# Edge messages summed per destination window on one Trainium2 core: strips and a fold replaced by one PSUM sum

## What is computed

```python
w_ij  = silu(edge_feats @ rad_W1 + rad_b1) @ rad_W2 + rad_b2
w_ij += silu(chi_scalar @ sph_W1 + sph_b1) @ sph_W2 + sph_b2
q_i = (node_feats @ Wq)[receivers];  k_j, v_j = (node_feats @ Wk)[senders], (node_feats @ Wv)[senders]
alpha = (q_i * w_ij * k_j).sum(axis=-1) / sqrt(16) * cutoffs      # per head: 8 heads of 16
out = segment_sum(alpha * v_j, receivers, num_segments=n_nodes) / 16
x = layernorm(x + out)
```

## Time and profile before

| | us |
|---|---|
| median of three runs (2751.88 to 2758.18) | 2755.45 |
| the profiled execution's own time | 2762.11 |
| its span, from the first to the last instruction | 2760.2 |
| TensorE busy (matmuls) | 1905.8 |
| TensorE's weight loads, which overlap matmuls | 1496.6 |
| VectorE busy | 1581.1 |
| GpSimd busy | 1537.5 |
| ScalarE busy | 712.5 |

### The profile page before, as it was taken

How to read it: one execution, slowest core, us unless ns; L and a number is a source line. 1 busy time by engine, 2 the same in 40 slices (tenths; PEclk the granted TensorE clock), 3 DMA queues, 4 the chain that set the end, 5 groups by cost and what they waited for, 6 DMA issues and landing times.

```text
span 2760.2 us, 40664 instructions
## 1 busy us (share of the span) xinstructions
PE 1905.8 (69%) x14110; PEld 1496.6 (54%) x14110; DVE 1581.1 (57%) x4221; ACT 712.5 (26%) x1030; POOL 1537.5 (56%) x1626
## 2 busy tenths in 40 slices
PE   6457666666677666766667677777677777777777
PEld 5345545555455455555555555555555555555555
DVE  3256555555555555555565565565565555655558
ACT  3222222222222222222222222222222222222224
POOL 5545555555555555555556555556555565555561
PEclk8677887778777787777777877777777777777778
DMA  7534443434344434434344444344344344344441
GB/s 247 172 117 126 119 126 113 126 111 129 113 127 114 125 116 122 128 113 129 111 127 132 120 129 133 117 131 133 116 132 133 115 133 133 114 134 131 121 130 48
DMA packets 166897, 348.12 MB, mean 126 GB/s; under 512 B 60797, under 2 KB 71912, under 8 KB 166696
## 3 DMA queue, kind: packets, MB, share of 16 engines
q0 software_dynamic: 76928, 209.56, 26.7%
q1 hardware_dynamic: 88358, 132.90, 14.7%
q10 hardware_dynamic: 1410, 3.07, 0.4%
HBM read 330.44 MB, written 14.95 MB: 125 GB/s over the span
## 4 chain that ended last, share of the span: by engine, by line
PE 36%; another core or an unknown queue 23%; DVE 20%; issue 19%; DVEq 1%; ACT 1%; DMA 0%; ACTq 0%; SPq 0%
PE bank L739 20%; DVE t L1049 5%; PE bank L782 4%; PE bank L757 4%; PE hidden L716 3%; PE bank L729 3%; DVE oh L940 2%; DVE ot L934 2%; DVE msg L1069 2%; DVE part L964 2%; DVE accT L990 2%; DVE t L1036 1%; PE hidden L325 1%; PE bank L465 1%
## 5 line engine op out<-in xcount | busy, mean ns | idle before, releaser
L701 POOL DMA_INDIRECT kvt<-kvtab,srcS x1584 | 1501.1, 948 | 1151.0 <-DVE msg L1069 688.1
L828 ACT ACTIVATE hs<-hidden,B 128x1024 f32<-128x1024 f32 x404 | 427.2, 1108 | 1639.2 <-remote 997.4
L739 PE MATMUL bank<-W2r,hs 128*128 128x128 f32 x3224 | 631.8, 357 | 25.2 <-ACT hs L828 17.5
L739 PEld LDWEIGHTS bank<-W2r,hs 128*128 128x128 f32 x3224 | 543.7, 255 | 128.6 <-issue 98.2
L739 PE MATMUL bank<-W2s,hs 128*128 128x128 f32 x3224 | 570.7, 335 | 5.9 <-issue 5.6
L739 PEld LDWEIGHTS bank<-W2s,hs 128*128 128x128 f32 x3224 | 541.6, 253 | 5.4 <-issue 5.1
L1036 DVE TENSOR_TENSOR t<-bank,kvt 128x512 f32<-128x512 f32 x395 | 271.8, 688 | 435.5 <-remote 249.6
L757 PE MATMUL bank<-msg,oh 128*32 128x128 f32 x3200 | 209.7, 341 | 413.5 <-issue 251.6
L757 PEld LDWEIGHTS bank<-msg,oh 128*32 128x32 f32 x3200 | 76.2, 121 | 623.4 <-issue 518.9
L1049 DVE TENSOR_TENSOR t<-bank,t 128x512 f32<-128x512 f32 x402 | 275.9, 686 | 238.0 <-remote 227.7
L782 PE MATMUL bank<-cS,part 128*128 128x32 f32 x704 | 152.1, 303 | 308.7 <-DVE part L964 303.8
(11 more groups left out here) (130 smaller groups left out, 680.2 us busy)
## 6 DMA issues: line engine op xcount, KB each, us to landing
dbt<-dst SPq DMA_DIRECT2D x102, 512.0 KB, 5.6
eft<-in_ef SPq DMA_DIRECT2D x102, 512.0 KB, 6.9
kvt<-kvtab,srcS POOLq DMA_INDIRECT x1584
qwt<-qtab SPq DMA_DIRECT2D x202, 32.0 KB
kvtab<-kvt SPq DMA_DIRECT2D x24, 256.0 KB, 2.0
qtab<-qx SPq DMA_DIRECT2D x12, 384.0 KB
out<-partn SPq DMA_DIRECT2D x48, 64.0 KB
accT<-in_xT SPq DMA_DIRECT2D x5, 512.0 KB
```

Of the source, the lines that this page charges most:

```text
L701: pool.indirect_dma_start(kvt[:, (g - HX) % KS, t, :], None, kvtab, bass.IndirectOffsetOnAxis(ap=srcS[:, g * TG + t:g * TG + t + 1], axis= ...
L739: m = pe.matmul(WB[g % 2][:, t * D:(t + 1) * D], hs[:, g % HS, j, t * 128:(t + 1) * 128], w2[:, :], start=(g < 2 and j == 0 and t == 0), s ...
L828: act.activation(hs[:, 2 * p % HS:2 * p % HS + n, j, :], hidden[:, 0:2 * n, :].rearrange("p (a j) f -> p a j f", j=2)[:, :, j, :], ACT.Sil ...
```

## The change

Every group is scattered as the last one was. The messages are the stationary operand (128 edges x 128 features), the one-hot matrix moves (32 columns), and the four tiles sum into one region of PSUM, 128 features x 32 nodes (`sums`). `accumulate` waits for the scatter instead of the fold, scales by 1/64 and adds. The strips, their copies in SBUF (`part`), the fold and its constant go; `collect` and `late_collect` remain for the 48 groups that norm nodes, with half the width, and the semaphore `m_part` counts these alone. The order of what remains is as before.

```diff
@@ scat, scat_whole, fold_tiles (TensorE)
+            def sums(g):
+                return strips(g)[:, 2 * D:2 * D + W]
+
             def scat(g):
                 pe.wait_ge(m_msg, g + 1)
...
                 for t in range(TG):
-                    m = pe.matmul(strips(g)[32 * t:32 * t + W, 0:D], oh[:, g % WS, t, :], msg[:, g % MS, t, :],
-                                  start=True, stop=True)
+                    m = pe.matmul(sums(g), msg[:, g % MS, t, :], oh[:, g % WS, t, :],
+                                  start=(t == 0), stop=(t == TG - 1))
                 if g in use_n:
...
-            def fold_tiles(g):
-                pe.wait_ge(m_part, g + 1)
-                pe.matmul(strips(g)[:, 2 * D:2 * D + W], parts(g), fold,
-                          start=True, stop=True).then_inc(m_fold, 1)
...
-                if g >= 3:
-                    fold_tiles(g - 3)
...
             scat(NE - 3)
             scat(NE - 2)
-            fold_tiles(NE - 3)
-            fold_tiles(NE - 2)
             scat_whole(NE - 1)
@@ late_collect (ScalarE)
             def late_collect(g):
+                c = use_n[g]
                 act.wait_ge(m_sc, g + 1)
-                if g >= 2:
-                    act.wait_ge(m_fold, g - 1)
...
+                act.activation(partn[:, c % 2, :], strips(g)[:, D:2 * D], ACT.Copy).then_inc(m_part, 1)
...
-                if LC <= g - 4 < NE - 1:
+                if g - 4 in use_n and g - 4 >= LC:
                     late_collect(g - 4)
@@ collect, accumulate (VectorE)
             def collect(g):
+                c = use_n[g]
                 dve.wait_ge(m_sc, g + 1)
-                if g >= 2:
-                    dve.wait_ge(m_fold, g - 1)
...
-                    dve.tensor_copy(partn[:, c % 2, :], strips(g)[:, 0:2 * D]).then_inc(m_part, 1)
-                else:
-                    dve.tensor_copy(part[:, g % 2, :], strips(g)[:, 0:D]).then_inc(m_part, 1)
+                dve.tensor_copy(partn[:, c % 2, :], strips(g)[:, D:2 * D]).then_inc(m_part, 1)
...
-                dve.wait_ge(m_fold, g + 1)
                 if g >= 1:
                     dve.wait_ge(m_acc, g)
-                dve.tensor_tensor(accT[:, bass.ds(at, W)], accT[:, bass.ds(at, W)], strips(g)[:, 2 * D:2 * D + W],
-                                  ALU.add).then_inc(m_acc, 1)
...
                 dve.wait_ge(m_sc, g + 1)
+                if g in use_n and g >= LC:
+                    dve.wait_ge(m_part, use_n[g] + 1)
                 dve.scalar_tensor_tensor(accT[:, bass.ds(at, W)], strips(g)[:, 2 * D:2 * D + W], 1.0 / 64,
                                          accT[:, bass.ds(at, W)], ALU.mult, ALU.add).then_inc(m_acc, 1)
...
-                if 0 <= g - 2 < LC:
+                if g - 2 in use_n and g - 2 < LC:
                     collect(g - 2)
```

More of the change, by code:

```diff
@@ L157, in gnn_program @@
         npass = sb("npass", [1, 1], i32)
-        cS = sb("cS", [128, 1 + W + 3 + 256 + W], f32)
+        cS = sb("cS", [128, 1 + W + 3 + 256], f32)
         pidx = cS[:, 0:1]
@@ L162, in gnn_program @@
         centre = cS[:, 4 + W:4 + W + 128]
-        fold = cS[:, 4 + W + 256:4 + W + 256 + W]
         eye = cS[:, 4 + W + 128:4 + W + 256]
@@ L204, in gnn_program @@
             sem(f"m_{n}") for n in ("t1", "t2", "rd", "al", "msg", "sc", "acc", "up")]
-        m_part, m_fold, m_bias = sem("m_part"), sem("m_fold"), sem("m_bias")
+        m_part, m_bias = sem("m_part"), sem("m_bias")
         m_cut = sem("m_cut")
@@ L593, in gnn_program @@
         oh = sb("oh", [128, WS, TG, W], f32)
-        part = sb("part", [128, 2, D], f32)
-        partn = sb("partn", [128, 2, 2 * D], f32)
+        partn = sb("partn", [128, 2, D], f32)
         hs = sb("hs", [128, HS, 2, G], f32)
@@ L639, in store @@
                 sp.wait_ge(m_y, c + 1)
-                sp.dma_start(out[c * 128:(c + 1) * 128, :], partn[:, c % 2, D:2 * D]).then_inc(m_out[c % 2], 16)
+                sp.dma_start(out[c * 128:(c + 1) * 128, :], partn[:, c % 2, :]).then_inc(m_out[c % 2], 16)
             def rows(b):
@@ L770, in scat_whole @@
                         pe.wait_ge(m_msg, g + 1)
-                    m = pe.matmul(strips(g)[:, 2 * D:2 * D + W], msg[:, g % MS, t, :], oh[:, g % WS, t, :],
+                    m = pe.matmul(sums(g), msg[:, g % MS, t, :], oh[:, g % WS, t, :],
                                   start=(t == 0), stop=(t == TG - 1))
                 m.then_inc(m_sc, 1)
[L775 to L778, removed]
-            def fold_tiles(g):
-                pe.wait_ge(m_part, g + 1)
-                pe.matmul(strips(g)[:, 2 * D:2 * D + W], parts(g), fold,
-                          start=True, stop=True).then_inc(m_fold, 1)
             l1(0)
@@ L853, in square @@
             def square(c):
-                g = at_n[c]
-                act.wait_ge(m_part, g + 1)
+                act.wait_ge(m_part, c + 1)
                 if c >= 1:
                     act.wait_ge(m_sq, c)
-                act.activation(sq[:, 0, :], partn[:, c % 2, D:2 * D], ACT.Square, scale=D ** -0.5,
+                act.activation(sq[:, 0, :], partn[:, c % 2, :], ACT.Square, scale=D ** -0.5,
                                accum_out=ss[:, c:c + 1]).then_inc(m_sq, 1)
@@ L865, in scale_by @@
             def scale_by(c):
-                act.activation(partn[:, c % 2, D:2 * D], partn[:, c % 2, D:2 * D], ACT.Copy,
+                act.activation(partn[:, c % 2, :], partn[:, c % 2, :], ACT.Copy,
                                scale=rs[:, c:c + 1]).then_inc(m_y, 1)
             def late_collect(g):
+                c = use_n[g]
                 act.wait_ge(m_sc, g + 1)
-                if g >= 2:
-                    act.wait_ge(m_fold, g - 1)
[L873 to L877, removed]
-                else:
-                    act.activation(part[:, g % 2, :], strips(g)[:, 0:D], ACT.Copy).then_inc(m_part, 1)
+                if c >= 2:
+                    act.wait_ge(m_out[c % 2], 16 * (c // 2))
+                act.activation(partn[:, c % 2, :], strips(g)[:, D:2 * D], ACT.Copy).then_inc(m_part, 1)
             for g in range(NE + 12):
@@ L954, in collect @@
             def collect(g):
+                c = use_n[g]
                 dve.wait_ge(m_sc, g + 1)
-                if g >= 2:
-                    dve.wait_ge(m_fold, g - 1)
[L958 to L961, removed]
-                    dve.tensor_copy(partn[:, c % 2, :], strips(g)[:, 0:2 * D]).then_inc(m_part, 1)
-                else:
-                    dve.tensor_copy(part[:, g % 2, :], strips(g)[:, 0:D]).then_inc(m_part, 1)
+                if c >= 2:
+                    dve.wait_ge(m_out[c % 2], 16 * (c // 2))
+                dve.tensor_copy(partn[:, c % 2, :], strips(g)[:, D:2 * D]).then_inc(m_part, 1)
             def first_guess(c):
@@ L1106, in gnn_program @@
                 dve.reciprocal(rs[:, c:c + 1], var[:, c:c + 1]).then_inc(m_rr, 1)
-            accumulate_whole(NE - 1)
+            accumulate(NE - 1)
             dve.wait_ge(m_acc, NE)
@@ L1157, in feat @@
         return a.reshape(ng, G, R).transpose(0, 2, 1)
-    cst = np.zeros((128, 1 + W + 3 + 256 + W), np.float32)
+    cst = np.zeros((128, 1 + W + 3 + 256), np.float32)
     cst[:, 0] = np.arange(128) // NPART
@@ L1164 @@
     cst[:, 4 + W + 128:4 + W + 256] = np.eye(128)
-    cst[:, 4 + W + 256:] = np.tile(np.eye(W), (128 // W, 1)) / 64.0
     w1 = np.concatenate([arr(L0_gnn_rad_W1), arr(L0_gnn_sph_W1)] * 2, 0)
```

## The result

The changed kernel takes 2925.15 us (median of four runs, 2919.83 to 2955.51); the kernel before took 2753.66 (2750.28 to 2758.18) with a fourth run, made beside it. The ratio is 1.063, with a 95% interval of 1.057 to 1.069: **slower by 171 us**, outside the range of 2500 to 2900, where 2657 was forecast.

The account below looks back on a forecast made before the run. No engine was full; an order of waits bound the kernel, TensorE's signals coming late during gathers. 2762.1 us - 99 (0.97 x 102 locked pairs) + 1 (last groups) = 2664, less 6.7 for the median: 2657; range 2500 to 2900.

Parts of the forecast that it names:

- the locked pair: Two groups in the later stretch, 12.8 us, 102 such pairs; the next odd product was to start 0.97 us earlier.
- GpSimd's rival: GpSimd's gathers become the bound as messages come 2 us sooner: pairs of 11.5 us, 2430 us, chance 0.08.
- The wait moves whole: Rival of no change: earlier gathers hold layer 2's signal by just what the copy's absence gives; 2755 us, chance 0.08.
- The slower rival: TensorE's loop of product, accumulate, scatter and layer 2 becomes the bound through the longer scatter: 2885 us, chance 0.34.
- Its other sign: Sign that TensorE's loop is the bound: pairs of 13.1 us and more late in the kernel.
- The scatter's price: TensorE, scatter's start to layer 2: 1.83 us at 1.2 GHz, 0.92 at 2.4; +1.07 and +0.49 us a pair.
- Removed work: Strip copies off VectorE, 0.42 us a pair; folds off TensorE, 0.29 us on the even group's path.
- The unlocked pair: Two groups in the earlier stretch, 13.56 us, some 93 pairs; product waits 3.78 us for a late signal; change put at 0.
- the text on the fold: Part on the removed fold matmuls: 0.29 us off the even group's path; in the odd one only the wait before.
- messages that follow the reduce without a wait: Sign of a right forecast: on VectorE, messages start after the reduce without the 2.71 us of waiting.
- VectorE's waits gathered at: Sign of a right forecast: VectorE's waiting collects before the weight product (L1036); no size given.
- the two that were about the rate: Signs of a right forecast: over 130 products in 800 us late, pairs near 11.9 us; GpSimd's wait for messages shorter.

Follow-up runs that it names:

- A: Changed kernel with one wait put back: VectorE waits for the scatter's signal ahead of the cutoff, where the copy stood; 2721.21 us, ratio 0.990.
- E: Kernel before, with only the copy of the strips moved behind the messages, which no longer wait for the scatter's signal; 3066.39 us, ratio 1.115.
- I: Changed kernel with one signal of layer 1 for two groups and gathers waiting once a pair for layer 2's signal; 2608.07 us, ratio 0.951.
- J: Kernel before with one signal of layer 1 for two groups and gathers waiting once a pair for layer 2's signal; 2605.09 us, ratio 0.952.
- D: Changed kernel without the gathers after the first ring of 15 groups; 1813.28 us.
- C: Kernel before without the gathers after the first ring of 15 groups; 1710.45 us.
- K: Changed kernel with gathers waiting once a pair for layer 2's signal, layer 1's four signals left; 2606.47 us, ratio 0.945.
- B: Kernel before with four matmul rows of the new form added to each scatter on TensorE; 2850.46 us, ratio 1.037.

## Why the prediction was wrong

- **The step that failed** is in the sum of the locked pair: "If the signal is let out when it is today (1433.05), it starts near 1433.15 instead of 1434.12: **-0.97**." The signal came at 1433.05 because the burst had ended, and the burst had ended because the messages, which release gathers, stood behind the copy's wait. The same sum brought the messages 2.14 us forward (1433.51 to 1431.37) and left the end of the burst where it was. With earlier messages the gathers no longer came in eights with one pause a pair: some bursts joined and held the signal longer, others split, and +1.11 a late pair was measured. A did it backwards (a wait given back, -204 us), E forwards (a wait taken out, +318).
- The text had the cause and did not carry it over. It read that the signals "are let out when a burst of them ends", and against GpSimd's rival it said that "with no pause in the gathers the late signals lose the moment at which they are let out". That sentence spoke against the forecast as well. "The wait moves whole" was the nearest case; the wait did not only move, it grew.
- **The slower rival** had the sign and nearly the time (2885), by a mechanism that carries little of it here: TensorE is busy 67%, where it asked for over 78, and with the scatter as it is A is faster than before and I equals J. Its other sign, pairs of 13.1 and more late in the kernel, came true (13.91) by another cause. The cost of the longer scatter shows in D, where no gathers run.
- **The scatter's price was right.** From the scatter's start to layer 2 it is 1.70 us at 1.2 GHz (1511.83 to 1513.53) and 0.92 at 2.4 GHz (1501.18 to 1502.10), against 1.83 and 0.92 put. The stretches that give the clock (last columns: clock, DMA share, GB/s):

```profile
1501.20:1502.10 0.90, 0.90 (x13) 0.90 (x9) 0.86 (x2) 0.00 (x0) 0.84 (x1) 1.00 0.41 105
...
1511.90:1513.60 1.70, 1.70 (x9) 1.70 (x9) 1.63 (x6) 0.32 (x1) 0.00 (x0) 0.50 0.44 127
```

The Trainium skill, "TensorE: Matmul & The Clock Gate", section "LDWEIGHTS (loading the stationary operand)", gives a load's time as its columns over 1.2 GHz; 0.85 us for eight such loads is the prediction's estimate from that. At 2.4 GHz the trace is near it (0.92); at 1.2 GHz it is twice that (1.70), and the measurement decides.

The prediction adds that by that price its forecast would be some 100 us lower. By its own sum it would not: there the locked product waits for the signal until 1433.15, later than the 1432.06 at which its work is done, so the scatter's price does not enter.

- **Removed work was right.** VectorE's busy time fell by 74.5 us (1581.1 to 1506.6), 0.37 a pair against 0.42 put; the accumulate takes 184 ns against 0.19 us; folds and strip copies are gone. With the pause put back (A) the late pair takes 12.80 us, as in the kernel before: there the removed work and the longer scatter together are worth nothing.
- **The unlocked pair** was put at 0, between -0.4 and +1.1; +0.35 was measured (118 to 115 products). Its sum takes 0.49 off for the folds, where the text on the fold gives 0.29 and names no second term.
- Of the signs named, "messages that follow the reduce without a wait" and "VectorE's waits gathered at" the weight product came true, with the opposite time; the two that were about the rate, over 130 products and a shorter wait of GpSimd, did not.

## What to carry to other kernels

A wait can be doing a job for another engine: before one is counted as a gain, follow what the waiting instruction releases, here gathers, during which the very signals that the next step waits for come late. If a pause is needed, place it where it is cheapest, on the engine that must pause and on the signal that is late; that took either kernel 5% below the one before, and then the change was worth nothing. A price of removed or added work that is right, and is not on the path, forecasts nothing.

## What had not been expected of the hardware

- TensorE's semaphore updates can come late while gathers run, by 6.7 us in the pair shown (layer 2 over at 1504.13, its update at 1510.80), and three came within 0.25 us once the packets had stopped. VectorE's signal of the messages, over at 1503.46 (1502.77 + 0.69) in the same burst, had reached GpSimd by 1503.77. Over the changed kernel from 400 to 2400 us every recorded update of VectorE and ScalarE follows the end of its instruction by at most 13 ns; without gathers (C) nine in ten of layer 2's do so within 15 ns.
- Not every signal of TensorE is late, so "late while gathers are in flight" is too wide a rule. In the rows of K layer 2 ends at 1610.21 (1608.51 + 1.70) amid gathers, and its product starts at 1610.32. The late ones are mostly those behind layer 1: in the changed kernel from 400 to 2400 us the median time from layer 2's end to its product is 0.11 us in the groups without layer 1 before them and 2.07 us in the others (1.90 us with one signal of layer 1). What in layer 1, or in the gathers, holds these signals back was not tried.
- A gather's row ends before its packets do: the last row of the burst ends at 1508.48, the packets at 1509.99. The Trainium skill, "Perfetto Trace Analysis", section "DMA Instruction — SWDGE (GPSIMD)", says that such a row ends when the descriptors are made, not when the data has moved; the trace agrees.
- Still open: why four matmul rows more a scatter cost some 100 us in B, while A, whose scatter is longer too, but which has neither folds nor copies, is some 27 us faster than before.
